# Folded value weights in plain fp32 on the quarters of the TensorE array, from unsplit values

## What is computed

```python
q = x @ Wq.T
kv = context @ Wkv.T                     # k, v: 16 heads of 64
sim = einsum('bhid,bhjd->bhij', q, k) * SCALE
attn = softmax(where(mask, sim, max_neg))
out = einsum('bhij,bhjd->bhid', attn, v)
return out.transpose(...).reshape(B, Nq, 1024) @ Wout.T + b_out
```

## Time and profile before

| | |
|---|---|
| median of 3 runs | 1264.33 us (1264.31 to 1264.49) |
| span of the profiled execution | 1262.7 us |
| PE busy | 1233.2 us, 98% |
| DVE busy | 873.9 us, 69% |
| POOL busy | 630.9 us, 50% |
| ACT busy | 569.3 us, 45% |

### The profile page before, as it was taken

One profiled execution on the slowest core, in us unless ns is written; L12 is line 12 of the kernel. 1 busy time (PEld: TensorE's weight loads), 2 busy tenths in 40 slices (PEclk: granted clock), 3 DMA queues, 4 the chain that ended last, 5 costly groups with the idle time before them and its releaser, 6 DMA issues.

```text
span 1262.7 us, 22568 instructions
## 1 busy us (share of the span) xinstructions
PE 1233.2 (98%) x8080; PEld 1117.3 (88%) x8080; DVE 873.9 (69%) x1694; ACT 569.3 (45%) x1117; POOL 630.9 (50%) x986
## 2 busy tenths in 40 slices
PE   8988999999999999999999999988999999999998
PEld 7877999999999999999999999877798899899888
DVE  5557888888888888888888888888534323422435
ACT  2134555546555555465555654555423312421420
POOL 3245766756767667667676675665322112202201
PEclk9999999999999999999999999999999999999999
DMA  9921111102111111021111110230121021012001
GB/s 276 223 61 34 43 34 51 51 26 59 34 43 44 34 51 51 26 59 35 43 43 34 51 51 26 63 105 26 61 99 49 20 67 67 1 67 67 1 1 35
DMA packets 117474, 69.98 MB, mean 55 GB/s; under 512 B 74098, under 2 KB 114803, under 8 KB 117364
## 3 DMA queue, kind: packets, MB, share of 16 engines
q1 hardware_dynamic: 115332, 67.87, 18.2%
q10 hardware_dynamic: 2032, 0.66, 0.3%
HBM read 42.29 MB, written 26.22 MB: 54 GB/s over the span
## 4 chain that ended last, share of the span: by engine, by line
PE 88%; DVE 3%; issue 1%; ACT 1%; POOL 1%; POOLq 0%; DVEq 0%
PE ob L137 7%; PE ob L138 7%; PE ob L139 7%; PE sim L138 7%; PE sim L137 7%; PE sim L139 7%; PE pw L435 4%; PE pt L484 4%; PE pw L137 3%; PE pw L138 3%; PE pw L139 3%; PE pw L387 3%; PE pt L139 2%; PE pt L138 2%; PE pt L137 2%; PE pw L411 2%
## 5 line engine op out<-in xcount | busy, mean ns | idle before, releaser
L1584 POOL TENSOR_TENSOR w_lo<-w_raw,w_hi 128x2048 fp32r<-128x2048 f32 x16 | 73.8, 4612 | 222.4 <-ACT w_hi L1524 169.3
L137 PE MATMUL ob<-b_hi,pT_hi 128*128 128x256 f32 x512 | 152.5, 298 | 3.8 <-DVE pT_lo L850 3.8
L138 PE MATMUL ob<-b_lo,pT_hi 128*128 128x256 f32 x512 | 143.8, 281 | 0.0
L139 PE MATMUL ob<-b_hi,pT_lo 128*128 128x256 f32 x512 | 143.5, 280 | 0.0
L943 POOL TENSOR_TENSOR prob<-prob,rz 128x512 f32<-128x512 f32 x128 | 131.0, 1045 | 10.3 <-DVE rz L791 10.3
L706 ACT ACTIVATE prob<-prob 128x512 f32<-128x512 f32 x128 | 80.7, 631 | 110.6 <-DVE prob L843 110.0
L838 DVE TENSOR_REDUCE mx<-sim 128x8 f32<-128x512 f32 x128 | 87.8, 686 | 35.9 <-PE sim L139 34.8
L137 PEld LDWEIGHTS ob<-b_hi,pT_hi 128*128 128x128 f32 x512 | 96.8, 189 | 8.6 <-DVE pT_lo L850 7.9
L137 PE MATMUL sim<-a_hi,tT_hi 128*128 128x512 f32 x256 | 103.6, 405 | 0.0
L618 ACT ACTIVATE x<-h,nmr,rstd 128x256 f32<-128x256 f32 x128 | 76.2, 596 | 58.3 <-POOL nmr L864 53.5
L138 PE MATMUL sim<-a_lo,tT_hi 128*128 128x512 f32 x256 | 101.3, 396 | 0.0
(11 more groups left out here) (245 smaller groups left out, 3860.3 us busy)
## 6 DMA issues: line engine op xcount, KB each, us to landing
xraw<-in_x SPq DMA_DIRECT2D x16, 512.0 KB, 4.0
kv_scratch<-stage SPq DMA_DIRECT2D x32, 256.0 KB, 3.6
x_scratch<-x SPq DMA_DIRECT2D x64, 128.0 KB, 1.7
out_x<-o_sb SPq DMA_DIRECT2D x64, 128.0 KB, 1.7
w_raw<-in_L_ffn_experts_inter SPq DMA_DIRECT2D x8, 1024.0 KB, 5.0
w_raw<-in_L_ffn_experts_out SPq DMA_DIRECT2D x8, 1024.0 KB, 7.7
kraw<-kv_scratch SPq DMA_DIRECT2D x32, 128.0 KB, 3.0
vraw<-kv_scratch SPq DMA_DIRECT2D x32, 128.0 KB, 3.0
```

The costliest lines, as they stand in the source:

```text
L137: pe.matmul(out, lh, rh, start=first, stop=False)
L138: pe.matmul(out, lh, rl, start=False, stop=False)
L139: return pe.matmul(out, ll, rh, start=False, stop=last)
```

## The change

- Values are loaded unpadded and unsplit, a batch ahead, into one of two buffers `vraw[:, e, head, key]`, by one DMA. Partitions 0 to 63 hold heads 0 to 7, partitions 64 to 127 heads 8 to 15; the value rows of Wkv and the columns of Wout are loaded in that order. The splits by ACT and POOL and their semaphores go.
- `wox` is kept unsplit, copied by DVE in setup; ACT's part of it goes. Wout comes by four DMAs in pieces of 256 bytes, the value half of Wkv by two DMAs for each of its two groups.
- B is one plain fp32 matmul a head, 64 rows by 64 columns by 256, at the quarter given by the head's partitions and by the half of the output's partitions.
- B0 and B1 are made together at PE's place 8 of slot 0, B2 and B3 together at place 3 of slot 1. B0 now holds pairs 0 and 1, B1 4 and 5, B2 2 and 3, B3 6 and 7. So the first half of P times B waits for B2, the second for B3. ACT makes `b_hi` of B0 at place 0 of slot 1.
- Some buffers move, as `hT` and `w2_hi` lie over others.

```diff
     ORDER = {
-        "G": ((0, 4), (0, 8), (0, 8)), "B0": ((0, 7), (0, 8), (1, 0)),
-        "B1": ((0, 7), (1, 0), (1, 0)), "GT": ((1, 1), (1, 3), (1, 3)),
-        "B2": ((1, 3), (1, 5), (1, 8)), "B3": ((1, 5), (1, 6), (1, 9)),
+        "G": ((0, 4), (0, 8), (0, 8)), "B0": ((0, 8), (1, 0), (1, 0)),
+        "B1": ((0, 8), (1, 0), (1, 0)), "GT": ((1, 1), (1, 3), (1, 3)),
+        "B2": ((1, 3), (1, 5), (1, 8)), "B3": ((1, 3), (1, 6), (1, 9)),
...
+    TOGETHER = {"B0": "B1", "B2": "B3"}
...
-            need(sp, "v_lo_made", it + 1)
-            load_kv(sp, vraw, 1, it + 1, "v_loaded")
+            need(sp, "prep_made", number(it - 1, last_of("B0", "B1", "B2", "B3")))
+            v_of = kv_scr[1, it + 1] if isinstance(it, int) else kv_scr[1, bass.ds(it + 1, 1), :, :, :].rearrange("o p r j -> (o p) r j")
+            sp.dma_start(vraw[:, (e + 1) % 2, :, :], v_of).then_inc(s["v_loaded"], 16)
...
+        if name in TOGETHER.values():
+            return
         b = batch_of(name, it)
         pw = pws[bank_of(name)]
+        mates = (name, TOGETHER[name]) if name in TOGETHER else (name,)
...
-        for back, other in [before_on_bank(it, name)] + [(0, x) for x in OPERANDS.get(name, ())]:
+        for back, other in [before_on_bank(it, x) for x in mates] + [(0, x) for x in OPERANDS.get(name, ())]:
...
-            need(pe, "v_hi_made", b + 1)
-            need(pe, "v_lo_made", b + 1)
+            need(pe, "v_loaded", 16 * (b + 1))
             for r in range(2):
-                pr = 2 * i + r
-                last = three_passes(pe, pw[:, r * C:(r + 1) * C], (v_hi[:, pr, :], v_lo[:, pr, :]),
-                                    (wox_hi[:, pr, :], wox_lo[:, pr, :]), True, True)
+                for g, mate in enumerate(mates):
+                    for o in range(2):
+                        d, keys, h = slice(g * NKV, (g + 1) * NKV), slice(o * NKV, (o + 1) * NKV), 2 * (i + r) + o
+                        last = pe.matmul(pws[bank_of(mate)][keys, r * C:(r + 1) * C], vraw[d, q, h, :], wox[d, h, :],
+                                         start=True, stop=True)
+                    if r == 1 and g == 0:
+                        last.then_inc(s["prep_made"], 1)
         last.then_inc(s["prep_made"], 1)
...
-            prep_done(pe, it, last_of("B0", "B1") if h == 0 else last_of("B2", "B3"))
+            prep_done(pe, it, last_of("B0", "B2") if h == 0 else last_of("B1", "B3"))
...
-        if slot == 3 and within(it + 1):
-            need(act, "v_loaded", 32 * (it + 2))
-            if within(it):
-                need(act, "prep_made", number(it, last_of("B0", "B1", "B2", "B3")))
-            act.activation(v_hi[:, :, :], vraw[:, :, :], ACT.Copy).then_inc(s["v_hi_made"], 1)
...
-        if slot == 3 and within(it + 1):
-            need(pool, "v_hi_made", it + 2)
-            pool.tensor_tensor(v_lo[:, :, :], vraw[:, :, :], f32(v_hi[:, :, :]), ALU.subtract).then_inc(s["v_lo_made"], 1)
...
-                    sp.dma_start(wout_raw[:, :, :], t["L0_xattn_Wout"].rearrange("(m p) n -> p m n", p=P)).then_inc(loaded["wout"], 16)
+                    for m in range(MC):
+                        for half in range(2):
+                            sp.dma_start(wout_raw[:, m, :].rearrange("p (i g d) -> p g i d", g=2, d=NKV)[:, half],
+                                         t["L0_xattn_Wout"][m * P:(m + 1) * P, half * W:(half + 1) * W].rearrange("p (i d) -> p i d", d=NKV)
+                                         ).then_inc(loaded["wout"], 16)
...
+            if kind == "wox":
+                last = dve.tensor_copy(wox[:, 2 * it[1]:2 * it[1] + 2, :], b[:, :].rearrange("p (r c) -> p r c", c=C))
```

More of the change, by code:

```diff
@@ L160, in setup_and_attention @@
     wqx = k.sb("wqx", [P, PAIRS, C + 1])
-    wox_hi = k.sb("wox_hi", [P, PAIRS, C], F32R)
-    wox_lo = k.sb("wox_lo", [P, PAIRS, C], F32R)
+    wox = k.sb("wox", [P, PAIRS, C])
+    k.sb("hT_lo1_room", [P, PAIRS, C])
     bq = k.sb("bq", [P, MC])
@@ L169, in setup_and_attention @@
     kraw = k.sb("kraw", [P, PAIRS, P])
-    vraw = k.sb("vraw", [P, PAIRS, P])
+    k.sb("x2T_lo_room", [P, PAIRS, P])
     g_sb = k.sb("g_sb", [P, 2 * C + 2 - P])
@@ L193, in setup_and_attention @@
         "prep_made", "prep_hi", "prep_split", "prep_copied", "state_ready", "st_prod", "r_prod", "r_summed", "wv_split", "g_split",
-        "v_hi_made", "v_lo_made",
         "tr_made", "tr_hi", "tr_taken", "xb_ready",
@@ L537, in pe_slot @@
         n = 4 * it + slot
-        prep = lambda place: [pe_prep(pe, x, j, par(0)) for x, j in at("pe", slot, place, it)]
+        prep = lambda place: [pe_prep(pe, x, j, par(it - j)) for x, j in at("pe", slot, place, it)]
         if has_sim:
@@ L600, in prep_views @@
             return pw[:, :], half(a_hi, i // 2)[:, i % 2, :], half(a_lo, i // 2)[:, i % 2, :]
-        return (pw[:, :].rearrange("p (r c) -> p r c", r=2), b_hi[:, 2 * i:2 * i + 2, :],
-                b_lo[:, 2 * i:2 * i + 2, :])
+        pair = i % 2 * (PAIRS // 2) + i // 2 * 2
+        return (pw[:, :].rearrange("p (r c) -> p r c", r=2), b_hi[:, pair:pair + 2, :],
+                b_lo[:, pair:pair + 2, :])
     def act_prep(act, name, it):
@@ L810, in dve_slot @@
         if (it, slot) == (NB - 1, 0):
-            need(dve, "v_lo_made", NB)
             ff["dve_free"](dve)
@@ L993, in setup_and_attention @@
               wv, wk, wq_hi, wq_lo, woc, bvbc, bkbc, bprime, boutbc, ident, blockmask,
-              wqx, wox_hi, wox_lo, bq, bvsum, mask_scr, epsc,
-              xraw, kraw, vraw, s["x_loaded"], wvT, wv_hi, wv_lo, s["wv_split"], len(FIRST_PREPS), first_prep, xT_parts)
+              wqx, wox, bq, bvsum, mask_scr, epsc,
+              xraw, kraw, s["x_loaded"], wvT, wv_hi, wv_lo, s["wv_split"], len(FIRST_PREPS), first_prep, xT_parts)
     b_hi = k.sb("b_hi", [P, PAIRS, C], F32R)
@@ L1006, in setup_and_attention @@
     b_lo = k.sb("b_lo", [P, PAIRS, C], F32R)
-    v_hi = k.sb("v_hi", [P, PAIRS, P], F32R)
-    v_lo = k.sb("v_lo", [P, PAIRS, P], F32R)
+    vraw = k.sb("vraw", [P, 2, PAIRS, NKV])
+    k.sb("w2_hi1_room", [P, PAIRS, P])
     prob = k.sb("prob", [P, 2, KEYS])
@@ L1080, in setup @@
 def setup(nc, t, k, kv_scr, NB, S, C, NKV, MC, PAIRS, wv, wk, wq_hi, wq_lo, woc, bvbc, bkbc, bprime, boutbc, ident,
-          blockmask, wqx, wox_hi, wox_lo, bq, bvsum, mask_scr, epsc,
-          xraw, kraw, vraw, x_loaded, wvT, wv_hi, wv_lo, wv_split, n_preps, first_prep, xT_parts):
+          blockmask, wqx, wox, bq, bvsum, mask_scr, epsc,
+          xraw, kraw, x_loaded, wvT, wv_hi, wv_lo, wv_split, n_preps, first_prep, xT_parts):
     NCTX = NB * NKV
@@ L1146, in operands_taken @@
         return max(items.index((kind, m, x)) for kind, x in (("ctxT", h), ("wkvT", ch // 4)) for m in range(MC)) + 1
-    SPLITS = ("ctxT", "wkvT", "xT", "wox")
+    SPLITS = ("ctxT", "wkvT", "xT")
     col = lambda i: slice(i * P, (i + 1) * P)
@@ L1156, in dest @@
             return wkvT_hi[:, it[1], c], wkvT_lo[:, it[1], c]
[L1157 to L1160, removed]
+        return xT_parts(it[1])[1:]
     def source(u):
@@ L1178, in load_ctx @@
             sp.dma_start(ctx_raw[:, q, :], ctx_tiles[:, q, :]).then_inc(ctx_loaded[h], 16)
+        wkv_values = t["L0_xattn_Wkv"][PAIRS * P:2 * PAIRS * P, :].rearrange("(g i d) c -> g d i c", g=2, d=NKV)
         def load_wkv(g):
             q = slice(4 * g, 4 * g + 4)
-            sp.dma_start(wkv_raw[:, q, :], wkv_chunks[:, q, :]).then_inc(wkv_loaded[g], 16)
+            if g < PAIRS // 4:
+                sp.dma_start(wkv_raw[:, q, :], wkv_chunks[:, q, :]).then_inc(wkv_loaded[g], 16)
+            else:
+                for half in range(2):
+                    sp.dma_start(wkv_raw[half * NKV:(half + 1) * NKV, q, :],
+                                 wkv_values[half, :, 4 * g - PAIRS:4 * g - PAIRS + 4, :]).then_inc(wkv_loaded[g], 16)
         load_ctx(0)
@@ L1259, in _ @@
         pool.memset(kraw[:, :, :], 0.0)
-        pool.memset(vraw[:, :, :], 0.0)
         for i in range(2):
@@ L1306, in _ @@
             elif kind == "wkvT":
-                pe.wait_ge(wkv_loaded[it[2]], 16)
+                pe.wait_ge(wkv_loaded[it[2]], 16 if it[2] < PAIRS // 4 else 32)
                 for i in range(4):
@@ L1315, in _ @@
             elif kind == "wox":
-                pe.wait_ge(loaded["wout"], 16)
+                pe.wait_ge(loaded["wout"], 32 * MC)
                 for r in range(2):
@@ L1319, in _ @@
                         last = pe.transpose(b[:, r * C + m * P:r * C + (m + 1) * P],
-                                            wout_raw[:, m, col(2 * it[1] + r)], ident[:, :])
+                                            wout_raw[:, m, col(2 * it[1] + r)],
+                                            ident[:, :])
             else:
@@ L1374, in _ @@
             dve.wait_ge(made, u + 1)
-            if kind == "wvT":
+            if kind == "wox":
+                last = dve.tensor_copy(wox[:, 2 * it[1]:2 * it[1] + 2, :], b[:, :].rearrange("p (r c) -> p r c", c=C))
+            elif kind == "wvT":
```

(6 more changed lines are left out.)

## The result

| | before | after |
|---|---|---|
| median | 1264.41 us (1264.31 to 1265.05) | 1310.47 us (1306.21 to 1313.22) |
| span of the profiled execution | 1262.7 us | 1308.9 us |

What follows compares the result with a forecast made beforehand. PE was taken to set the pace, busy 98% of the span. Batches add 14 x 4.4 + 2 x 3.3 = 68 us: 1262.7 + 68 + 0.3 + 1.6 = about 1332 us, range 1300 to 1348 us.

Steps and rivals of the forecast that it cites:

- likeliest case: B's matmuls overlap two heads at once, 1.95 us a pair of B tiles: 1322 to 1348 us, chance 0.45.
- rival 1: All four quarters work at once, 0.87 us a pair of B tiles; waits cost 2.7 us a batch: 1308 us, chance 0.35.
- The step that failed: In B's matmuls, a head's adjacent records on one quarter hold up those behind, so two heads overlap: 1.95 us a pair.
- The chain worked out from there: DVE's work from B0's copy to B2's split runs late, so slot 1's pB starts at 327.95, not 323.57: 4.4 us a batch.
- PE work added: 16 heads a batch, two records each, 0.217 us a step; a pair between 0.87 and 3.47 us, taken as 1.95.
- Switching the array: Four changes a batch between whole and quartered array: taken as nothing, at most 0.16 us each, 10 us in all.
- (a): At PE's place 3 of slot 1, B2 and B3 wait for GT's copy: some 2 us, 14 times.
- (b): In slot 1, the first half of pB waits for B2's split by DVE: some 1 us, 16 times.
- (c): In slot 0, pB's second half waits for pT_lo, since B0 no longer lies between: 0.2 us.
- Rival 3: The waits for GT's copy and B2's split don't bind; with four quarters at once 1247 us, chance 0.15.
- The clock: Idle PE at place 3 may lower the granted clock: up to 1.4 us a batch, 22 us, in the range alone.
- What costs nothing: DVE, ACT and POOL work, value loads and setup DMAs hold PE nowhere; Wout's loading in setup taken as 0.3 us.

Runs made afterwards that it cites:

- e6: The changed kernel with the two heads of one quarter directly behind each other in a pair of B tiles: 1310.56 us, ratio 1.0363.
- e8: e4 with ScalarE copying GT ahead of the exp and Wout loaded by four DMAs: 1263.14 us, ratio 0.9985.
- e1: The changed kernel with ScalarE copying GT at place 1, ahead of the exp of slot 1's first half: 1320.36 us, ratio 1.0434.
- e3: The changed kernel with the edits of e1 and e2 together: 1280.34 us, ratio 1.0123.
- e4: e2 with B0 and B1 made at place 7 of slot 0, again ahead of pB's second half: 1270.0 us, ratio 1.0039.
- e9: e1 with B2 copied at ACT's place 3 and split at DVE's place 5, heads dealt as in the changed kernel: 1275.85 us, ratio 1.009.
- e2: The changed kernel with heads dealt so B0 and B1 hold pairs 0 to 3; pB's first half in slot 1 waits for B1: 1297.32 us.

## Why the prediction was right, and where not

The measured 1310 us lie in the range and on the forecast's side, 22 us under the forecast of 1332 and outside the 1322 to 1348 of its likeliest case. The range holds only because it took in rival 1, whose mechanism is the one that the traces show and whose time, 1308 us, is 2 us off. That it is so close is in part luck: the sum of rival 1 has 16 times 2.7 us and nothing for switching or clock, where the trace has 2.97 us in twelve intervals, less in the first ones, and 4 falls of the clock.

- **The step that failed** is the one that made the forecast rather than rival 1: "The second cannot start before the first has streamed, and the next head, behind it, can start only together with that second one. That overlaps two heads, not four". A pair was put at 1.95 us; it takes 1.02 us, and e6 shows that the order of the heads does not bring it near that. The chain worked out from there stood. Measured from pB's first half in slot 0, rival 1 had GT's copy end at 322.46 - 312.63 = 9.83 us and pB of slot 1 at 13.67; the trace has 444.37 - 434.68 = 9.69 and 13.93. (One slip changes nothing: in rival 1 PE stands at place 3 from 316.62 + 3.26 = 319.88, not 320.0.)
- **PE work added.** Two records a head and steps of 0.217 us: right (0.215). Four at once was put at 0.87 us; it is 1.02 us, the first step 0.27 us and the last 0.33.
- **Switching the array.** I took nothing, with 0.16 us a switch as upper end; it costs that and a little more. In the rows shown the pair starts 0.21 us (438.01 - 437.80) behind a pB matmul whose step is 0.12, lasts 1.02 us, and the second sim matmul comes 0.34 us behind the first, where a step inside sim is 0.23. That is 0.09 + 1.02 + 0.11 = 1.22 us for four steps of 0.215, 0.86: 0.36 us a pair, 0.18 us a switch. The change of form alone is not the reason. On the whole array, in the kernel before, four fp32 transposes start at 319.87, the first fp32r matmul behind them at 320.22, and the second is

```profile
320.43 0.28 PE L138 MATMUL pw<-wox_lo,v_hi 128*128 128x256 f32 x1
```

so it is 0.56 us for four steps of 0.11 and one of 0.12, and nothing is lost. The rule of the Trainium skill ("TensorEngine Tiling (Array Packing)", Key Properties) that a change of tiling mode drains the engine agrees with that. Of the 1.08 us a batch that four at once should save PE, 2 x (1.41 - 1.22) = 0.38 us are left, and e8 shows 0.17.
- **The waits.** (a) at place 3 for GT's copy: forecast about 2 us, 14 times; 1.8 us, 13 times, and 0.8 us in the first batch, ahead of the window. (b) for B2's split: about 1 us, 16 times; 0.97 us in the batches at full clock, less where the clock fell, more in the last two. (c) pB's second half in slot 0 for pT_lo: 0.2 us; it starts at 436.40, 0.22 us behind 436.06 + 0.12, where it was due. The mechanism of (a) and (b), DVE's chain set off late by B0's copy, was argued from an unbroken row of work; e1, e3, e4 and e9 show it.
- **Rival 3** (the waits don't bind, 1247 us) fell as an account of this kernel. With the waits undone (e8) it would still have been too low by 16 us, for PE's saving is 0.2 us a batch and not 1.08.
- **The clock** was put in the range alone, with up to 1.4 us a batch: 1.1 us, in 4 batches of the profiled run, and in 12 of e6's with the same stand.
- **What costs nothing.** Right: PE waits for none of it, and the first interval from G to G is 54.96 us, 54.81 before. The 0.3 us can't be told from nothing: this interval lies between 54.4 and 56.4 us in the experiments, whatever the number of DMAs.

The rule I weighed at the quarters, in "TensorE: Matmul & The Clock Gate" of the Trainium skill, Part 3, has two sides. Starts about 4 ns apart on different tiles: within a four 6 to 7 ns in most here, one of 35 ns in some, and 13 in e6. Strict order of start and end: I read from it that adjacent records of one quarter hold up the others, and the measurement decides against that reading: 1.04 us in e6, where it would give 2.8.

## What to carry to other kernels

Before making an operation cheaper by joining two groups, ask what lay between them: here one place later on PE was worth 1.4 us a batch, as much as the whole pair of tiles. Read the chain through the engines that are not the bottleneck; an engine with 13% to spare can still be late at one point of every batch, and moving an entry or two in the orders of ACT and DVE can then win far more than lighter work on PE (35 us in e9, with no work taken away). Mend all points at which one lateness is met together, since one alone may win nothing (e1) where both win much (e3).

## What the runs showed of the hardware

- Plain fp32 matmuls of 64 rows by 64 columns, two records each, run on all four quarters at once in both orders of the heads tried: 16 records in 1.02 us (1.04 in e6), 0.215 us for each four of 256 columns. That is 16 heads in 2.05 us; 24 fp32r matmuls on the whole array with zero-padded values took 2.82.
- A change between quarters and whole array costs about 0.18 us each way in the pair worked out above, 0.7 us a batch by that, most of what the quarters save.
- After stands of 1.79 us the granted clock sometimes fell to 1.2 GHz for 3.41 us, at a price of 1.1 (after) to 1.6 us (e2) a fall: 4 of 13 times after, 12 of 13 in e6, 1 of 13 in e2; and 13 of 14 times around stands of 2.1 us (e1). So the length of the stand alone does not decide it; what does stays open.
